# Reordered queues in the start of an adaLN block: scale rows and columns, shift columns, GpSimd's remainders and second-norm moments

## The reference

```python
mod = (_silu(c) @ wmod).reshape(2, 6, 1, -1)          # sa, ca, ga, sb, cb, gb
h = _layernorm(x) * (1 + ca) + sa
x = x + ga * (h @ (weight * block_mask).T + bias)     # 512 -> 512, mask in blocks of 32x32
h = _layernorm(x) * (1 + cb) + sb
h1, h3 = lora_linear(h, w1, A1, B1), lora_linear(h, w3, A3, B3)   # 512 -> 1376
x = x + gb * lora_linear(silu(h1) * h3, w2, A2, B2)               # 1376 -> 512
```

## Time and profile before

| | before |
|---|---|
| median of 3 runs | 258.7 us (258.66 to 258.78) |
| the profiled execution | 259.44 us |
| its span in the trace | 257.7 us |
| PE busy | 242.3 us (94%) |
| DVE busy | 133.7 us (52%) |
| ACT busy | 85.5 us (33%) |
| POOL busy | 43.1 us (17%) |
| mean granted clock of TensorE | 0.982 |

### The profile page before, as it was taken

The page is one execution under the profiler, slowest core; times in us unless marked ns, Lnnn a source line. Parts: engine busy times, 40 slices in busy tenths (PEclk is TensorE's granted clock), DMA queues, the critical chain, the costliest instruction groups (busy, mean ns, idle before and its releaser), DMA issues.

```text
span 257.7 us, 3366 instructions
## 1 busy us (share of the span) xinstructions
PE 242.3 (94%) x1205; PEld 189.4 (73%) x1205; DVE 133.7 (52%) x230; ACT 85.5 (33%) x157; POOL 43.1 (17%) x58
## 2 busy tenths in 40 slices
PE   7999399988999999999999999999999999999990
PEld 6667256666678888888888878888888888888770
DVE  2778747899896977855555523641122102221144
ACT  2346229385552223275475312011101101010100
POOL 2002804911210111430330100230000000000012
PEclk9999869999999999999999999999999999999998
DMA  5999999220244232142313710057000000000004
GB/s 151 360 391 396 394 405 325 58 81 3 81 122 125 48 116 84 42 122 84 117 45 101 56 10 0 1 28 178 0 0 0 0 3 0 0 1 3 0 0 163
DMA packets 14565, 26.37 MB, mean 102 GB/s; under 512 B 1618, under 2 KB 3538, under 8 KB 14420
## 3 DMA queue, kind: packets, MB, share of 16 engines
q1 hardware_dynamic: 14112, 26.01, 33.4%
q10 hardware_dynamic: 436, 0.15, 0.2%
HBM read 23.26 MB, written 2.10 MB: 98 GB/s over the span
## 4 chain that ended last, share of the span: by engine, by line
PE 82%; DVE 10%; issue 3%; ACT 2%; POOL 1%; DVEq 0%; ACTq 0%; POOLq 0%
PE up_a L1256 15%; PE up_b L1256 15%; PE acc L1282 8%; PE acc L1284 8%; PE acc L1283 8%; PE up_a L1265 7%; PE up_b L1265 7%; PE acc L1210 3%; PE acc L1290 2%; DVE stats L754 2%; PE side L1238 2%; PE side L1210 2%; ACT wa_hi L585 1%; DVE wa L898 1%; PE side L1243 1%
## 5 line engine op out<-in xcount | busy, mean ns | idle before, releaser
L1014 DVE TENSOR_TENSOR g<-up_b,g 128x512 f32<-128x512 f32 (+1 forms) x22 | 15.2, 690 | 71.3 <-PE up_b L1265 71.3
L1282 PE MATMUL acc<-w_hi,g_hi 128*128 128x512 f32 (+1 forms) x88 | 34.9, 396 | 0.0
L1284 PE MATMUL acc<-w_hi,g_lo 128*128 128x512 f32 (+1 forms) x88 | 34.8, 395 | 0.0
L1283 PE MATMUL acc<-w_lo,g_hi 128*128 128x512 f32 (+1 forms) x88 | 34.7, 395 | 0.0
L723 ACT ACTIVATE g<-up_a 128x512 f32<-128x512 f32 (+1 forms) x22 | 13.1, 597 | 58.7 <-PE up_a L1265 58.7
L731 ACT ACTIVATE g_hi<-g 128x512 fp32r<-128x512 f32 (+1 forms) x22 | 13.9, 632 | 55.2 <-DVE g L1014 55.2
L914 DVE SCALAR_TENSOR_TENSOR raw<-side,raw 128x512 f32<-128x512 f32 (+2 forms) x31 | 20.2, 677 | 18.9 <-PE side L1238 11.4
L669 ACT ACTIVATE w_hi<-raw 128x512 fp32r<-128x512 f32 (+2 forms) x33 | 20.3, 625 | 16.5 <-DVE raw L914 16.5
L1256 PE MATMUL up_a<-ht_hi,w_hi 128*128 128x512 f32 (+1 forms) x88 | 24.5, 400 | 0.3 <-ACT w_hi L669 0.3
L517 POOL TENSOR_TENSOR xt<-work,xt 128x512 f32<-128x512 f32 x5 | 6.8, 1379 | 103.9 <-DVE work L929 103.9
L1256 PE MATMUL up_b<-ht_hi,w_hi 128*128 128x512 f32 (+1 forms) x88 | 23.8, 393 | 0.0
(11 more groups left out here) (152 smaller groups left out, 328.8 us busy)
## 6 DMA issues: line engine op xcount, KB each, us to landing
raw<-in_ffn SPq DMA_DIRECT2D x33, 256.0 KB, 2.7
xt<-in_x SPq DMA_DIRECT2D x8, 256.0 KB, 9.6
wmod_sb<-in_wmod SPq DMA_DIRECT2D x2, 1024.0 KB, 14.0
wmod_sb<-in_wmod SPq DMA_DIRECT2D x1, 2048.0 KB, 15.1
out<-xt SPq DMA_DIRECT2D x8, 256.0 KB, 2.9
mask_sb<-in_mask SPq DMA_DIRECT2D x4, 256.0 KB, 6.1
ca_sb<-in_wmod_ca SPq DMA_DIRECT2D x4, 256.0 KB, 6.3
wa<-in_weight SPq DMA_DIRECT2D x4, 256.0 KB, 6.6
```

The lines of the kernel that those rows point to most:

```text
L1014: nc.vector.tensor_tensor(g[0:w], up_b[0:w], g[0:w], ALU.mult).then_inc(g_ready, 1)
L1282: nc.tensor.matmul(acc[t][:], hi, down_hi[j][0:w], start=(j == 0), stop=False)
L1283: nc.tensor.matmul(acc[t][:], hi, down_lo[j][0:w], start=False, stop=False)
L1284: last = nc.tensor.matmul(acc[t][:], lo, down_hi[j][0:w], start=False, stop=(j == HT - 1))
```

## The change

Nothing is added or removed; instructions change places in the queues of SP, POOL, ACT, DVE and PE.

- SP: for chunks 1 to 3 the scale weights are loaded ahead of the mask.
- PE, chunk stage: `rows_ca(k + 1)` stands between the two halves of the first four products of chunk k, and `mask_blocks(k + 1)` with `columns_ca(k + 1)` right behind those four, ahead of the products with low x.
- DVE: the shift columns (`columns_sa`) stand ahead of the last of the four `moment_a`, no longer behind `norm_parts(0)`; `masked_weight_low(1, 1)` and `(1, 2)` move between and behind the moments.
- POOL: `x_low(1)` to `x_low(3)` wait for `norm_cols_ready`, the end of `norm_parts(0)`; `spread(0)` stands ahead of the two residual additions.
- DVE, second norm of batch 0: moments stand between the residual additions, the last one behind `centres`, and `merge(1)` moves ahead of `norm_parts(1)`.
- ACT: `weight_high(0)` stands ahead of `norm(0)` and `norm(1)`.
- DVE, first feed-forward step: `lora_part(2)` stands behind the two merges, no longer ahead of them.

```diff
             for k in range(KT):
-                sp.dma_start(mask_sb[:, k], mask[:, k]).then_inc(mask_loaded[k], 16)
+                if k == 0:
+                    sp.dma_start(mask_sb[:, k], mask[:, k]).then_inc(mask_loaded[k], 16)
                 sp.dma_start(ca_sb[:, k], wmod_ca[:, k]).then_inc(ca_loaded[k], 16)
+                if k:
+                    sp.dma_start(mask_sb[:, k], mask[:, k]).then_inc(mask_loaded[k], 16)
...
             root(NORM_A[0], slice(0, T))
+
+            pool.wait_ge(norm_cols_ready, 1)
             for k in range(1, KT):
                 x_low(k)
+            spread(0)
             for i in X1_POOL:
                 add_x1(i)
-            spread(0)
             root(NORM_A[1], slice(0, T))
...
             mod_evacuate()
+            weight_high(0)
             norm(0)
             norm(1)
-            weight_high(0)
             norm_rows_evacuate(1)
...
             masked_weight_low(1, 0)
-            for t in range(T):
-                moment_a(0, t)
+            moment_a(0, 0)
+            moment_a(0, 1)
             masked_weight_low(1, 1)
+            moment_a(0, 2)
+            columns_sa()
+            moment_a(0, 3)
+            masked_weight_low(1, 2)
             norm_parts(0)
-            columns_sa()
-            masked_weight_low(1, 2)
             uv_sum()
...
+            add_x1(0, 2)
+            moment_f(0)
+            add_x1(0, 3)
+            moment_f(1)
+            moment_f(2)
+            columns_f()
             centres()
+            moment_f(3)
             merge(0)
+            merge(1)
             norm_parts(1)
             norm(0, 2, ORDER[2])
             norm(0, 3, ORDER[3])
-            merge(1)
...
-            lora_part(2)
             for s in range(B * HT):
...
                 for at in pieces_up(s):
                     merge(PIECE[at])
-                if s == 1:
-                    lora_part(3)
+                if s < 2:
+                    lora_part(2 + s)
...
             for k in range(KT):
-                attend(0, k, 0, every)
+                attend(0, k, 0, first)
+                if k + 1 < KT:
+                    rows_ca(k + 1)
+                attend(0, k, 0, last_two)
                 if k + 1 < KT:
                     mask_blocks(k + 1)
-                    rows_ca(k + 1)
+                    columns_ca(k + 1)
                 attend(0, k, 2, every)
-                if k + 1 < KT:
-                    columns_ca(k + 1)
-                else:
+                if k + 1 == KT:
                     rows_sa()
                 attend(0, k, 1, every)
```

More of the change, by code:

```diff
@@ L967, in _, with moment_f @@
                 attn_gate(0, i)
[L968 to L971, removed]
+            def moment_f(i):
                 dve.wait_ge(*x1_done(i))
                 moment(NORM_F[0], i, xt[:, 0, ORDER[i]])
-                if i == 2:
-                    columns_f()
+            add_x1(0, 2)
[4 more added lines that the diff above has]
+            columns_f()
             centres()
+            moment_f(3)
             merge(0)
+            merge(1)
             norm_parts(1)
```

## The result

The changed kernel takes 255.97 us, median of 4 (255.88 to 256.3), against 258.74 us, median of 4 (258.66 to 260.46), for the kernel before. The ratio is 0.9879, 95% interval 0.9838 to 0.9921: 1.2% less. I had forecast 254.3 us, in a range from 252.4 to 256.4. So direction and range held, and the gain of 2.8 us is 1.6 short of the 4.4 that I had summed. The profiled execution took 255.88 us with a span of 254.1; before they were 259.44 and 257.7. Between the two traces the gain is thus 3.6 us. Of the four runs of the kernel before, three took 258.66 to 258.78 and one 260.46; the changed kernel's four lie within 0.42 us.

The account below looks back on a forecast made before the run. PE's 4.1 us wait before `uv`, caused by GpSimd's x_low holding DVE, plus slow clock, was taken as the bound. Terms -4.65 + 0 + 0.25 = -4.4, from the median of 258.7, gave 254.3 us, range 252.4 to 256.4.

Parts of the forecast that it names:

- What bound the kernel: PE's 4.1 us wait before `uv`: GpSimd's x_low holds two-SBUF-input DVE operations in norm_parts(0), delaying the shift-column copy; half clock follows.
- no exclusion to speak of: Rival, chance 0.17: x_low holds up no DVE work; turn_moments(0) at 32.15, attend_end(0) at 35.1, -6.0 and +0.25, 252.9 us.
- Chunk stage, -0.15 and worthless: PE's chunks shorten, but rows_sa waits for shift weights landing at 23.1: -0.15 us, lost at gate_rows(0)'s load.
- Shift columns and `uv`: Earlier DVE copy lets PE start `uv` at 27.45 without a wait; gate_rows(0) starts at 29.75, behind its weights.
- GpSimd behind the means: x_low after norm_parts(0): gates ready at 33.4, turn_moments(0) at 33.5, attend_end(0) from 41.08 to 36.4, -4.65 us.
- more exclusion: Rival, chance 0.15: x_low(3) gets in before lora_part(1); uv_split ends 36.9, attend_end(0) 37.2, -3.9 + 0.25, 255.0 us.
- Second norm, 0: From attend_end(0) to turn, new DVE order of additions, moments, merges: 0 us, bounds -0.5 and +0.5.
- small GpSimd operations hold the port to their end too: Rival, chance 0.07: batch 1's power operation delays the second residual addition, adding 0.5 us before turn; 254.8 us.
- `lora_part(2)`, +0.25: First feed-forward step: DVE waits for the merges' matmuls, weight_low ends later; +0.25 us, bounds -0.4 and +0.4.
- The sum: Whole kernel: -4.65 + 0 + 0.25 = -4.4, profiled 259.44 to 255.0; from the median of 258.7, 254.3 us.
- The clock: Forecast: no dip on PE. Rival, chance 0.10: idle pieces bring the lower level, 257.0 us at worst, 256.3 with shorter dip.

Follow-up runs that it names:

- experiment 2: Kernel before with only GpSimd's part: x_low(1) to x_low(3) wait for the end of norm_parts(0), spread(0) ahead of the additions; 254.94 us, ratio 0.9822.
- experiment 1: Kernel before with only DVE's new order up to uv_sum, the shift columns' copy ahead of the last first-norm moment; 258.03 us, ratio 0.9939.
- experiment 7: experiment 6 with x_low(1) and x_low(2) ahead of GpSimd's root and x_low(3) waiting for the gates; 254.25 us, ratio 0.98.
- experiment 3: Changed kernel with PE's chunk loop and SP's order of mask and scale loads undone; 255.98 us, ratio 0.9881.
- experiment 6: Kernel before with the chunk stage, shift columns and GpSimd's part, without the second norm's order and lora_part(2)'s new place; 255.19 us, ratio 0.9837.
- experiment 5: Changed kernel with the second norm's order on DVE and weight_high(0)'s place on ACT as before; 255.67 us, ratio 0.9854.
- experiment 4: Changed kernel with lora_part(2) back ahead of the two merges of the first feed-forward step; 255.56 us, ratio 0.9849.
- experiment 12: The kernel before run again, unchanged, for its own spread; 258.93 us, median of 10 runs, ratio to itself 0.9997.
- experiment 8: experiment 7 with gates_of(0) ahead of lora_part(0) on DVE; 253.98 us, ratio 0.9791.
- experiment 9: experiment 8 with x_low(3) waiting for lora_part(1) in place of the gates; 253.86 us, ratio 0.9788.
- experiment 10: experiment 9 with shift weights loaded ahead of batch 0's x, gate weights ahead of the first low-rank weights, gate_abs(0) earlier on ACT; 253.81 us, ratio 0.9802.
- experiment 11: experiment 10 with the chunk stage and the order of mask and scale loads as before; 253.72 us, ratio 0.9782.

## Why the prediction came out as it did

*What bound the kernel.* Right. The wait before `uv` was GpSimd's exclusion: taking `x_low` out of the way of three tiny operations (experiment 2) gives all of the gain and more (4.7 us against the kernel before of its session), moving the copy around them (experiment 1) only a third of that (1.65). The rival "no exclusion to speak of" is out by the 1.0 to 1.75 us that three operations took, and by experiment 7, where they took 0.29 to 0.74. One thing I had too narrow: I spoke of DVE operations with two SBUF inputs, but of the three in `norm_parts(0)` the CAST has one, and it was held as well (1.20 us before, 1.22 in experiment 1).

*Chunk stage, -0.15 and worthless.* That it is worthless is right (experiment 3), and the bound was the load, as said: 0.84 us of wait. The -0.15 didn't come: the load, which I took to land at 23.1 as before, landed at 11.5 + 12.3 = 23.8, and `rows_sa` started at 23.84, 0.30 us later than before.

*Shift columns and `uv`.* `uv` started at 27.94 in place of 27.45, for that load; `gate_rows(0)`, behind its own, at 29.74 where I had 29.75. What I didn't see is that the copy's move gives nothing beside GpSimd's (experiments 2 and 6). The reason isn't the load of the gate weights: `gate_rows(0)` starts at 30.53 in experiment 2 and at 30.21 in experiment 3, and `turn_moments(0)` at 33.57 and 33.69 all the same. It is the gates on DVE, queued behind `x_low`: PE's wait for them is 1.28 us in the changed kernel and shrinks to 0.43 and 0.87 us when PE comes later.

*GpSimd behind the means.* I had the gates ready at 33.4 and `turn_moments(0)` at 33.5; it started at 33.71. But one step failed, that DVE with `masked_weight_low(1, 3)` and `lora_part(1)` back to back keeps `x_low(3)` out: `x_low(3)` came in ahead, and the first of them took 1.75 us. That is the mechanism of the rival "more exclusion", at about half its price, and `attend_end(0)` came at 36.84 in place of 36.4 (the rival had 37.2): the term was -4.24, not -4.65. Half of the difference is that `turn_moments(0)` came 0.21 us later; the other half is between there and `attend_end(0)`, 3.13 us in place of 2.91, as `uv_split` ends at 36.69 behind the held operation.

*Second norm, 0.* It costs 0.25 in the traces and 0.3 in experiment 5, inside my bound of 0.5. My count gave `norm_parts(1)` 0.75 us behind `merge(1)`; its four operations took 1.05, beside small GpSimd operations. Two of the four are longer than before, L789 by 0.09 us and L796 by 0.14. The Trainium skill (SBUF — State Buffer, "SBUF: two separate sides") has the lock held for the whole instruction. The trace doesn't agree for small ones: L796 took 0.31 us inside a `spread` that runs from 47.74 for 0.61 us. And the rival "small GpSimd operations hold the port to their end too" falls: its second residual addition took 0.66 us at 42.02, inside the power operation that runs from 41.48 for 1.05 us.

*`lora_part(2)`, +0.25.* Right in mechanism and place; 0.43 in the traces, just outside my bound of 0.4, and 0.4 in experiment 4.

*The sum.* These three terms account for 0.4 + 0.25 + 0.2 = 0.85 us, of the 0.9 by which the profiled execution missed the 255.0 that I had for it. The other half of the miss (255.97 against 254.3) is a term that I didn't have: I took the gain off the median of 258.7, although the profiled execution that I had summed against was 0.7 above it, while after the change the two agree within 0.1. In the later sessions the kernel before had medians of 259.68, 259.52, 259.32 and 258.93 us; its runs spread over 1.9 us, the changed kernel's own over 0.4. The record shows what the difference goes with: the profiled execution has a mean granted clock of 0.982, and so has the slower kind of runs in experiment 12, while runs as short as 258.7 all have 0.987 to 0.989 there. The changed kernel took 255.88 to 256.3 us at 0.993 and at 0.997 alike. So what the lower clock cost differed from run to run before the change, and the runs at the median paid less of it than the trace that I summed against. Where in a short run the clock stays up longer isn't shown, as both traces are of long ones.

*The clock.* Right for the changed kernel: it stays up in its trace, with idle pieces of up to 1.36 us between 20 and 60 us. The rival isn't without ground, though: experiment 3 has pieces of the same length in its trace (1.37 us the longest), and two of its six runs, at 0.985 and 0.990, took 1.3 to 1.5 us more.

## What to carry to other kernels

A tiny operation on DVE can cost as much as the GpSimd operation that runs beside it: look for operations whose duration in one place is several times that in another, and put GpSimd's long two-input work where DVE has nothing to do that was seen to be held (two inputs in SBUF, or a CAST from SBUF to SBUF), not just somewhere else (experiment 7 against 6, 0.9 us). When a change has many parts, each has to be tried alone: here one part of seven gave more than all; the second norm's order with ACT's cost 0.3 us and the place of `lora_part(2)` 0.4; PE's chunk stage with SP's order stood behind a load that no reordering of compute could move; and the copy's move gave nothing that can be seen beside GpSimd's. And if the profiled execution isn't at the median, ask what differs (here the mean clock of each run says it) before taking a gain off the median.

The fastest versions are experiments 8 to 11, between 253.7 and 254.0 us and not told apart; against the kernel before, experiment 9's ratio is 0.9788, interval 0.9763 to 0.9813.

## What the runs showed of the hardware that I hadn't expected

- DVE operations in a row don't always keep GpSimd out: behind a gate operation that depended on another, `x_low(3)` got its turn (1.75 us for `masked_weight_low`), while in the trace of before a `spread` was kept waiting through two additions. In experiment 7 it got in between two that don't depend on each other, `masked_weight_low(1, 3)` (0.74 us) and `lora_part(1)` (1.91 us). What decides it isn't settled.
- In the trace of experiment 1 the granted clock fell to 0.50 behind an idle stretch of 2.7 us on PE, and in nine of its twelve runs the mean clock is low; in the changed kernel, with 1.36 us at most, it is low in none of four, in experiment 3, with 1.37, in two of six. The same kernel can have both. A fall costs part of the 3 us or so of work behind the wait, beside the wait's own length.
- The first chunk's start varies between 9.12 and 9.66 us over the fourteen traces taken. In kernels that wait for the shift weights' load it doesn't decide when `rows_sa` starts: in experiment 4 that is 23.94 after a first chunk at 9.12, in the changed kernel 23.84 after one at 9.43.
